# Elementwise work of a kernel's opening moved from VectorE to GpSimd, and the experts' weights loaded in four portions

## The reference, cut to what matters

```python
# x: 6250 x 256, src/dst/edge_type: 200,000 edges sorted by dst
h = layernorm(x)
msg = h[src] + relvectors[edge_type]                  # 16 relations
red = segment_sum(msg, dst, 6250)
x = x + gru_cell(red, h, w_ih, w_hh, b_ih, b_hh)      # 768 x 256 weights
z = layernorm(x)
idx = top_k(z @ Wg + bg, 2)                           # 8 experts
y_e = gelu(z @ W1[e] + b1[e]) @ W2[e] + b2[e]         # 256 -> 512 -> 256
x = x + sum of y_e over the two experts of each row
```

## Time and profile before

| | us |
|---|---|
| median of 3 runs | 1611.08 |
| lowest and highest of them | 1608.55, 1616.82 |
| the profiled execution, its own time | 1608.13 |
| its span, first to last instruction | 1606.3 |
| TensorE matmul busy | 1333.8 (83%) |
| VectorE busy | 1100.4 (69%) |
| GpSimd busy | 1034.2 (64%) |
| ScalarE busy | 708.4 (44%) |
| mean granted TensorE clock | 0.909 of full speed |

### The profile page before, as it was taken

How to read it: one execution, slowest core, us unless ns; L and a number is a source line. 1 busy time by engine, 2 the same in 40 slices (tenths; PEclk the granted TensorE clock), 3 DMA queues, 4 the chain that set the end, 5 groups by cost and what they waited for, 6 DMA issues and landing times. The chain is left out here.

```text
span 1606.3 us, 37371 instructions
## 1 busy us (share of the span) xinstructions
PE 1333.8 (83%) x12905; PEld 1025.3 (64%) x12905; DVE 1100.4 (69%) x3994; ACT 708.4 (44%) x1538; POOL 1034.2 (64%) x948
## 2 busy tenths in 40 slices
PE   1269999999989999989889998784653899999991
PEld 1235656666656666666667766564653799999991
DVE  7867677577777777778979888953545455555550
ACT  6334444444445554434433332221221676667660
POOL 2177777566777777676777777777773255555552
PEclk9959999999999999999998999686766899999996
DMA  9676544344554455444544544446652455555556
GB/s 304 175 214 197 153 127 114 109 132 133 138 146 137 132 148 143 123 115 142 145 132 146 146 133 112 113 120 211 236 119 60 100 101 94 95 94 96 94 80 179
DMA packets 136158, 220.43 MB, mean 137 GB/s; under 512 B 27761, under 2 KB 101046, under 8 KB 134688
## 3 DMA queue, kind: packets, MB, share of 16 engines
q0 software_dynamic: 63872, 123.12, 31.7%
q1 hardware_dynamic: 72096, 94.84, 19.7%
HBM read 169.05 MB, written 57.76 MB: 141 GB/s over the span
## 5 line engine op out<-in xcount | busy, mean ns | idle before, releaser
L667 POOL DMA_INDIRECT ring<-h_table,idx x728 | 727.2, 999 | 316.2 <-issue 254.8
L780 ACT ACTIVATE amat<-P 128x300 f16<-128x300 f32 (+3 forms) x608 | 230.6, 427 | 398.0 <-PE P L1642 396.2
L1655 PE MATMUL P<-hs,amat 128*126 128x512 f16 (+4 forms) x1323 | 356.9, 399 | 0.0
L721 POOL DMA_INDIRECT out_rows<-yo,xrows x112 | 176.5, 1576 | 162.4 <-DVE yo L1527 114.6
L1140 DVE TENSOR_SCALAR cone<-iota,comb 128x294 f16<-128x294 f16 (+3 forms) x840 | 258.2, 310 | 0.0
L1139 DVE TENSOR_SCALAR lone<-iota,slo 128x128 f16<-128x128 f16 x840 | 223.7, 267 | 15.7 <-PE P L1637 15.2
L1637 PE MATMUL P<-cone,lone 128*128 128x294 f16 (+3 forms) x840 | 164.6, 291 | 52.3 <-ACT amat L780 32.5
L1655 PEld LDWEIGHTS P<-hs,amat 128*126 128x126 f16 (+4 forms) x1323 | 160.7, 137 | 71.9 <-issue 8.2
L1518 DVE SCALAR_TENSOR_TENSOR gl<-gT,scales,gh 128x512 f16<-128x512 f32 x112 | 84.2, 752 | 126.1 <-ACT gh L904 126.1
L1869 PE MATMUL P<-xh,w_all 128*128 128x256 f16 x896 | 157.0, 274 | 0.0
L676 POOL DMA_INDIRECT expert_rows<-xrow,slots x100 | 121.6, 1216 | 54.3 <-issue 26.8
(11 more groups left out here) (240 smaller groups left out, 2666.3 us busy)
## 6 DMA issues: line engine op xcount, KB each, us to landing
raw<-in_L_ffn_W_dram SPq DMA_DIRECT2D x32, 512.0 KB
xrows<-expert_rows SPq DMA_DIRECT2D x56, 257.0 KB, 3.2
ring<-h_table,idx POOLq DMA_INDIRECT x728
w_parts<-parts SPq DMA_DIRECT2D x16, 512.0 KB
w_all<-w_parts SPq DMA_DIRECT2D x8, 1024.0 KB
h_in<-h_table SPq DMA_DIRECT2D x25, 250.0 KB
x<-in_x_dram SPq DMA_DIRECT2D x25, 250.0 KB
out_rows<-x SPq DMA_DIRECT2D x25, 250.0 KB
```

The costliest lines, as they stand in the source:

```text
L667: nc.gpsimd.indirect_dma_start(out=ring[:, r, j, :], out_offset=None, in_=h_dram, in_offset=bass.IndirectOffsetOnAxis(ap=idx[:, slot, g * ...
L721: nc.gpsimd.indirect_dma_start(out=out_dram, out_offset=bass.IndirectOffsetOnAxis(ap=xrows[:, b % XR, j, D:D + 1].bitcast(I32), axis=0), i ...
L780: nc.scalar.activation(amat[:, b % 2, :, s * aw:(s + 1) * aw], P[2 + g % 2][:, 0:HIS * aw].rearrange("p (h w) -> p h w", w=aw), ACT.Copy). ...
L1655: nc.tensor.matmul(both, amat[:, b % 2, hi, 0:used], hs[:, hi, :], start=(hi == 0), stop=False)
```

## The change

Two things are changed.

The first is in the opening. `rest(c)` for the chunks 0, 2 and 4, the chain of six that splits the relation vectors, and two of the three key instructions go to GpSimd. VectorE keeps the `bitwise_and`, which moves ahead of `bases()`. SyncE waits for the chunks in the same order, on either of two semaphores. GpSimd's new instructions stand between its two conversions and its wait for `s_bias`.

The second is the load of `w_all`. It is issued in four portions of two experts, at the tiles 21, 22, 23 and 24.

```diff
+POOL_RESTS = (0, 2, 4)
...
             for c in range(LN_CH + 1):
-                sp.wait_ge(s_rest1, c + 1)
+                if c in POOL_RESTS:
+                    sp.wait_ge(s_rest2, POOL_RESTS.index(c) + 1)
+                else:
+                    sp.wait_ge(s_rest1, c + 1 - sum(n < c for n in POOL_RESTS))
...
                 if i == FREE_TILE:
                     sp.wait_ge(head_free, 1)
                     sp.wait_ge(w_stored, 16 * WJOBS)
-                    for e in range(NE):
+                for e in range(NE * (i - FREE_TILE) // (TILES - FREE_TILE), NE * (i + 1 - FREE_TILE) // (TILES - FREE_TILE)):
+                    if e >= 0:
                         sp.dma_start(w_all[:, e, :], w_dram[e]).then_inc(w_loaded, 16)
...
@@ GpSimd, behind its two conversions
+            def pool_link(ins):
+                made[0] += 1
+                ins.then_inc(pool_chain, 1)
+                pool.wait_ge(pool_chain, made[0])
+
+            def rest(c):
+                pool.wait_ge(s_part1, c + 1)
+                at = hs[:, c * LN_J:c * LN_J + LN_J, :]
+                nc.gpsimd.tensor_tensor(at[:, :, D:PD], xc[:, c % XB, :, :], at[:, :, 0:D], ALU.subtract).then_inc(s_rest2, 1)
+
+            rest(0)
+            rest(2)
+            pool.wait_ge(s_rel, 16)
+            pool_link(nc.gpsimd.tensor_scalar(rel_rest, rel_raw, UP, None, ALU.mult))
+            for part in range(PARTS):
+                pool_link(nc.gpsimd.tensor_copy(rels[:, part, :], rel_rest))
+                if part + 1 < PARTS:
+                    pool_link(nc.gpsimd.tensor_tensor(rel_rest, rel_rest, rels[:, part, :], ALU.subtract))
+            rest(4)
+            pool.wait_ge(s_keys, 1)
+            nc.gpsimd.tensor_copy(slo[:, :], slo_i[:, :])
+            pool_link(nc.gpsimd.tensor_copy(comb[:, :], src_t[:, 0:HEAD * GC]))
+            nc.gpsimd.tensor_tensor(comb[:, :], comb[:, :], slo[:, :], ALU.subtract).then_inc(s_keys, 1)
...
@@ VectorE, small_weights
-                dve.wait_ge(s_rel, 16)
-                link(nc.vector.tensor_scalar(rel_rest, rel_raw, UP, None, ALU.mult))
-                for part in range(PARTS):
-                    link(nc.vector.tensor_copy(rels[:, part, :], rel_rest))
-                    if part + 1 < PARTS:
-                        link(nc.vector.tensor_tensor(rel_rest, rel_rest, rels[:, part, :], ALU.subtract))
+                dve.wait_ge(s_keys, 2)
...
@@ VectorE, the order of the opening
-            rest(0)
             edge_windows()
             rest(1)
...
-            rest(2)
...
-            rest(4)
             rest(5)
             rest(6)
+            dve.wait_ge(s_tr_out, RT)
+            nc.vector.tensor_scalar(slo_i[:, :], src_t[:, 0:HEAD * GC], 127, None, ALU.bitwise_and).then_inc(s_keys, 1)
             bases()
...
@@ VectorE, head_keys
-                link(nc.vector.tensor_scalar(slo_i[:, :], src_t[:, 0:n], 127, None, ALU.bitwise_and))
-                nc.vector.tensor_copy(slo[:, :], slo_i[:, :])
-                link(nc.vector.tensor_tensor(comb[:, :], src_t[:, 0:n], slo_i[:, :], ALU.subtract))
```

More of the change, by code:

```diff
@@ L451, in gnn_ffn_kernel @@
         names = """
-            s_const s_ones s_pads s_wnat s_weights s_rel s_ln_var s_ln_std s_ln_coef s_ln_h s_part1 s_rest1 s_natf
+            s_const s_ones s_pads s_wnat s_weights s_rel s_ln_var s_ln_std s_ln_coef s_ln_h s_part1 s_rest1 s_rest2 s_keys s_natf
             s_viol s_violb s_natd s_base s_based s_tr s_dst_out s_tr_out s_flag s_bias s_zero s_small s_init
@@ L463, in gnn_ffn_kernel @@
             tx_done xh_ready xl_ready w1_ready l1_done gelu_done g_high g_low l2_done y_out firsts_ready
-            out_written dve_chain late_chain
+            out_written dve_chain late_chain pool_chain
         """.split()
-        (s_const, s_ones, s_pads, s_wnat, s_weights, s_rel, s_ln_var, s_ln_std, s_ln_coef, s_ln_h, s_part1, s_rest1, s_natf,
+        (s_const, s_ones, s_pads, s_wnat, s_weights, s_rel, s_ln_var, s_ln_std, s_ln_coef, s_ln_h, s_part1, s_rest1, s_rest2, s_keys, s_natf,
          s_viol, s_violb, s_natd, s_base, s_based, s_tr, s_dst_out, s_tr_out, s_flag, s_bias, s_zero, s_small, s_init,
@@ L477, in gnn_ffn_kernel @@
          tx_done, xh_ready, xl_ready, w1_ready, l1_done, gelu_done, g_high, g_low, l2_done, y_out, firsts_ready,
-         out_written, dve_chain, late_chain) = [sem(n) for n in names]
+         out_written, dve_chain, late_chain, pool_chain) = [sem(n) for n in names]
         s_nat = [sem(f"s_nat{n}") for n in range(3)]
@@ L659, in _ @@
                 nc.gpsimd.tensor_copy(nat[:, c + 1, :, :], nat_i[:, c + 1, :, :]).then_inc(s_natf, 1)
+            made = [0]
+            def pool_link(ins):
[19 more added lines that the diff above has]
+            nc.gpsimd.tensor_tensor(comb[:, :], comb[:, :], slo[:, :], ALU.subtract).then_inc(s_keys, 1)
             pool.wait_ge(s_tr, 3 * RT + 6)
@@ L1100, in head_keys @@
             def head_keys():
-                n = HEAD * GC
-                link(nc.vector.tensor_scalar(slo_i[:, :], src_t[:, 0:n], 127, None, ALU.bitwise_and))
-                nc.vector.tensor_copy(slo[:, :], slo_i[:, :])
-                link(nc.vector.tensor_tensor(comb[:, :], src_t[:, 0:n], slo_i[:, :], ALU.subtract))
                 for first, end, k, aw, size, c in zone_batches():
```

## The result

| | before | changed |
|---|---|---|
| median of 20 runs each, us | 1612.32 | 1622.19 |
| the profiled execution, its own time | 1608.13 | 1625.48 |
| its span | 1606.3 | 1623.5 |
| start of `bases` | 57.12 | 62.70 |
| VectorE's last subtraction starts | 61.16 | 69.70 |

The account below looks back on a forecast made before the run. The prediction took GpSimd's first gathers, TensorE's work and GpSimd's last gathers as the bounding chain. Opening 4.45 less loads' 0.65 gave 3.8, on 1611.1 a forecast of 1614.9 us, range 1606.5 to 1620.5.

Parts of the forecast that it names:

- What bounds the kernel: Whole kernel: a chain of GpSimd's first gathers, TensorE's work, then GpSimd's gathers up to the last.
- The price of a `rest`: Opening: one `rest` on GpSimd takes 3.55 us, scaled from the CAST; bounds 1.89 and 4.6.
- The hold: Opening: a one-input VectorE instruction is held until the GpSimd instruction is through; forecast 1614.9 us, chance 0.40.
- Rival B: Opening: instructions with two SBUF inputs are held as well; 8.05 us there, 1618.5 in all; chance 0.22.
- ScalarE late at chunk 2: Opening: `rest(0)` holds a TENSOR_SCALAR, so ScalarE starts chunk 2 at 27.64 instead of 25.31, 2.3 late.
- ScalarE at chunk 6: Opening: `rest(4)` holds `first_targets` by 2.7 more, 4.7 in all; ScalarE's wait at 51.75 grows by as much.
- B's 1.2 for the mutual hold: Opening, under Rival B: GpSimd's `rest(4)` and VectorE's `rest(3)` also wait for each other, 1.2 us.
- Inside `bases`: Opening: GpSimd's key instructions hold one more TENSOR_SCALAR for 0.2 us; 2.2 under Rival B.
- First gather: End of the opening: 3.85 + 0.4 + 0.2 = 4.45 us later, near 76.7; Rival B has 8.05 in the opening.
- The gain of 0.65: Loop near 1140: splitting the weight loads lets GpSimd idle 0.30 instead of 0.95; bounds 0 to 1 us.
- a gather is late by a quarter as much, which the ring of two steps takes up: Loop, tiles 21 to 24: with 2 MB loaded at a time, gathers' lateness shrinks and buffering hides it.
- The sum: Whole kernel: 4.45 us lost in the opening less 0.65 gained by the loads, 3.8 us slower.

Follow-up runs that it names:

- e1: The changed kernel with all eight loads of the experts' weights at tile 21 again; ratio to the kernel before 1.0042, +6.5 us.
- e8: The kernel before with two memsets of idle memory on GpSimd ahead of its first gather; ratio 1.0046, +9.9 us, on another chip.
- e9: The kernel before with `wnat` and `bias_rows` laid behind `xc`, `small_weights` waiting for the transposes; ratio 0.9968, -6.7 us.
- e6: Kernel before, relation chain and keys on GpSimd only behind VectorE's last opening subtraction, `bitwise_and` behind `bases`; ratio 1.0011, +1.3 us, on another chip.
- e2: The kernel before with the loads of the experts' weights in four portions at tiles 21 to 24; ratio 1.0032, +5.1 us.
- e3: The kernel before with two experts' weights loaded at tile 21, two at 22, none at 23, four at 24; ratio 1.0006, 0.0 us.
- e4: e1 with GpSimd's key instructions kept back until VectorE's last opening subtraction is done; against the kernel before ratio 1.002, +3.6 us.
- e7: The kernel before with relation chain and keys on GpSimd as in the change, every `rest` on VectorE; ratio 1.0045, +8.6 us, on another chip.

## Why the prediction was wrong, point by point

**What bounds the kernel: right.** A first gather later by 7.6 and 7.9 made the kernel slower in e1 and e8, one earlier by 2.7 faster in e9, and VectorE's work behind the branch showed no gain in e6.

**The price of a `rest`: too low.** It was 4.05 and 4.08 in place of the 3.55 scaled from the CAST, and within the bounds. The Trainium skill (GPSIMD Engine Reference, section 3.1) has 4.497 us for an fp32 addition of this size; the rows, whose second input is float16, lie between. `rest(4)` took 4.70, as it started 0.77 ahead of the end of VectorE's `rest(3)` (47.25 + 2.29 = 49.54) and was held itself.

**The hold: the mechanism was right, its limit to one-input instructions was the step that failed.** The sentence "I take this to hold for the new ones" covered the TENSOR_SCALAR alone. Rival B, with a chance of 0.22, is what happened. Its signs all came: the SCALAR_TENSOR_TENSOR (3.93), the mutual hold of `rest(4)` and `rest(3)`, and the short instructions of `bases` held for 3.0 (69.70 less 62.70, against 61.16 less 57.12). The terms, forecast and measured:

- ScalarE late at chunk 2: 2.3, measured 2.5 (27.84 against 25.31).
- ScalarE at chunk 6: 4.7 late forecast, measured 57.76 against 51.75, 6.0 late. With B's 1.2 for the mutual hold it fits. Its wait itself grew from 1.37 to 5.21 and not "by as much", as ScalarE was already late when it began to wait.
- `bases`: near 61.5 forecast, 62.70 measured, 5.6 late in place of 4.25.
- Inside `bases`: 0.2 forecast, 3.0 measured; B had 2.2.
- First gather: 4.45 forecast, 8.05 by B (its terms add up to 7.95), 7.94 measured. That B is so near is partly luck: the last subtraction was 8.5 late, as the key instructions took 3.7 us (0.88 + 0.89 + 1.95) where B had 3.0, and the way from there to the first gather gave 0.6 back (10.5 us against 11.1).

The Trainium skill (SBUF — State Buffer, section "SBUF: two separate sides") states the rule as B used it, and these rows agree with it for TENSOR_TENSOR and SCALAR_TENSOR_TENSOR. TENSOR_SCALAR, with one input, it counts among those that contend in their faster modes, and the one at 49.46 was held too. BATCH_NORM_STATS2 wasn't held beside `rest(2)`, which the same section says of VectorE instructions with at most one SBUF input outside their faster modes. The trace of before held no case of a two-input instruction beside GpSimd, and so the rule deserved more than the chance that came from the missing row.

**The loads: the second step that failed.** The gain of 0.65 shows in no comparison. No row of GpSimd idles over 0.31 between 1125 and 1160 in the changed kernel, where the earlier trace rows has 0.95; but in e1 and e9, with all eight loads at tile 21, none does either. From the 664th gather to the last it took 94.1 us before, 93.2 and 93.9 in these two, 93.8 in the changed kernel and 94.9 in e2.

TensorE's wait of 11.58 did become shorter. Its timeline in the changed kernel, whose first portion was issued at 1119.14:

```profile
1118.45 0.82 PE L1611 MATMUL P<-onehot,ring 128*128 128x48 f16 x16 [4.39 <-DMA ring<-h_table,idx]
...
1133.19 0.82 PE L1611 MATMUL P<-onehot,ring 128*128 128x48 f16 x16 [5.80 <-DMA ring<-h_table,idx]
```

Only the second row answers to the 11.58. The first ended ahead of the load, and the kernel before has its twin ahead of its own loads of 1105.58:

```profile
1104.94 0.82 PE L1590 MATMUL P<-onehot,ring 128*128 128x48 f16 x16 [4.46 <-DMA ring<-h_table,idx]
```

What failed is "a gather is late by a quarter as much, which the ring of two steps takes up". TensorE waited 5.8 us with 2 MB under way, half of 11.58 and not a quarter. The ring takes it up only while GpSimd has further gathers ahead of it. At the last two steps there are none, and TensorE's lateness goes to the end. I had looked at the portion of tile 24, behind the gathers, and called nothing new of those at 22 and 23; the row at 1200.83 with its 3.78 us of slack was in the earlier trace rows and should have been held against the portion at 23. Measured: 3 us at the end, 5.1 [1.8, 8.5] in the time of e2. Of the 3, up to 1.7 are TensorE at the lower clock behind its wait, a term that the forecast didn't have.

**The sum.** 4.45 - 0.65 = 3.8 was forecast. The traces give 7.94 + 3 = 10.9, as the 0.65 can't be seen, and 9.9 was measured. The agreement is no closer than the loop's own spread. Even B, 1618.5, stayed below, for want of the loads' term. The range ended at 1620.5 for the same reason: no rival gave the loads a cost.

**Left open.** Why the loop up to the 664th gather took from 1026.0 to 1036.1 us with the same instructions in the same order isn't settled; the granted clock of the whole execution was 0.916 in the shortest (e9) and 0.894 in the longest (e3), which goes with it but doesn't show what comes first. The changed opening may have a share in it. In the 20 executions of the changed kernel and the 24 of e1 and e4 the granted clock was never above 0.899. In the 59 of the kernel before, e2 and e3 in the same rounds as e1 and e4 it was 0.900 or more in 22. No run tells whether the clock is lower because TensorE starts later, or what it costs. Nor is it settled which kinds of VectorE instruction are free of the hold, beyond BATCH_NORM_STATS2 and, in e7, a TENSOR_REDUCE that started at 27.51 beside GpSimd's TENSOR_SCALAR of 27.22 to 28.19 and took its usual 2.29.

## What to carry to other kernels

Moving elementwise work from VectorE to GpSimd isn't a trade of 2.3 us for 4.1 in parallel. While the GpSimd instruction ran, the next VectorE instruction of the kinds named above stood still, also a tiny one that another engine waited for. Place such work where VectorE waits for something else or runs statistics, or leave it. And a large load split into portions must be laid against the last use of the stream that it disturbs, not against the stretch where it now hurts: late gathers in the middle of the buffered loop cost nothing that e3 shows, while the same lateness in the last step but one went to the end.

## What the runs showed of the hardware

- VectorE and GpSimd held each other up. The rows: 0.17 of work that took 3.93 and 0.42 that took 4.29, each up to about the end of the other's instruction, and 0.66 on GpSimd that took 2.60, ending 0.53 behind the VectorE instruction beside it. A GpSimd operation on 16 partitions held VectorE too: the SCALAR_TENSOR_TENSOR at 39.65 took 0.50, and ended at 40.15 beside GpSimd's subtraction of 39.47 + 0.66 = 40.13.
- TensorE waited longer for gathered rows when plain loads were under way. Beside 8 MB the wait was 11.58 us, beside the first 2 MB 5.80 and beside the second 5.83 in the changed kernel. In the quiet stretch between 1160 and 1180 of the kernel before it was 4.69 and 4.33, and at the end of its loop the last rows were in use 5.2 us after their issue.
- After a wait of 4.98 us in e2 TensorE's granted clock was 0.76 over the next 8.4 us, and the same 68 matrix products took 7.32 us of busy time, against 5.58 at 1.00 in the kernel before.
